# Marking three adjacency visits by one operation each, in a graph-transformer block on one Trainium2 core

## What is computed

```python
def gnn_layer(x, W, b, src, dst):
    h = x @ W.T + b
    msgs = h[src]
    agg = segment_sum(msgs, dst, num_segments=1250)
    return relu(agg)
...
xn = layernorm(x)
x = x + gnn(xn, edges, W1, b1, W2, b2) + mix(xn, Wq, Wk, Wv, W1, W2)
x = x + ffn(layernorm(x), gate_weight, experts)
```

## Time and profile before

| | us |
|---|---|
| median of 3 runs | 469.77 |
| lowest, highest | 468.29, 471.64 |
| the profiled execution | 468.61 |
| span of its trace | 466.8 |

### The profile page before, as it was taken

The page is one execution under the profiler, slowest core; times in us unless marked ns, Lnnn a source line. Parts: engine busy times, 40 slices in busy tenths (PEclk is TensorE's granted clock), DMA queues, the critical chain, the costliest instruction groups (busy, mean ns, idle before and its releaser), DMA issues.

```text
span 466.8 us, 6816 instructions
## 1 busy us (share of the span) xinstructions
PE 451.0 (97%) x2424; PEld 360.6 (77%) x2424; DVE 320.9 (69%) x1104; ACT 150.6 (32%) x272; POOL 63.1 (14%) x90
## 2 busy tenths in 40 slices
PE   7999999999999999999999999999999998878995
PEld 3788778888888888888779999877777776655783
DVE  6995699899998988897752110444645666777972
ACT  4686453322323332332222110222133114551110
POOL 4088200000000000000004000002300000006642
PEclk9999999999999999999999999999999999999999
DMA  8902002911000000001200000002744449305891
GB/s 219 287 1 91 1 0 91 219 50 65 2 1 1 1 1 1 1 2 20 108 0 4 1 1 1 1 0 53 277 139 134 134 142 380 131 1 190 289 356 71
DMA packets 20846, 40.46 MB, mean 87 GB/s; under 512 B 2953, under 2 KB 3283, under 8 KB 20805
## 3 DMA queue, kind: packets, MB, share of 16 engines
q1 hardware_dynamic: 18549, 32.55, 22.4%
q0 software_dynamic: 2256, 7.39, 4.5%
HBM read 30.10 MB, written 10.31 MB: 87 GB/s over the span
## 4 chain that ended last, share of the span: by engine, by line
PE 86%; DVE 8%; ACT 2%; issue 1%; DMA 1%; SPq 0%; POOLq 0%; DVEq 0%
PE ps L736 46%; PE ps L1031 9%; PE ps L957 9%; PE ps L848 5%; PE ps L723 5%; PE ps L1167 2%; ACT scrap_a L1424 1%; PE ps L1048 1%; PE ps L1137 1%; DMA X<-in_x 1%; PE ps L880 1%; PE ps L770 1%; PE ps L984 1%; PE ps L1008 1%; PE ps L1078 1%
## 5 line engine op out<-in xcount | busy, mean ns | idle before, releaser
L1713 DVE TENSOR_SCALAR RING_D<-places,PLACES 125x170 bf16<-125x170 f16 (+1 forms) x239 | 63.5, 266 | 0.0
L1714 DVE TENSOR_SCALAR RING_S<-iota,HOME 125x128 bf16<-125x128 f16 x239 | 60.4, 253 | 0.0
L957 PE MATMUL ps<-AT,H1H 125*128 125x416 f32 (+1 forms) x108 | 38.0, 352 | 0.0
L957 PE MATMUL ps<-AT,H1L 125*128 125x416 f32 (+1 forms) x108 | 38.0, 351 | 0.0
L1031 PE MATMUL ps<-H2H,AT 125*125 125x512 f32 x90 | 36.1, 402 | 0.0
L1031 PE MATMUL ps<-H2L,AT 125*125 125x512 f32 x90 | 35.5, 394 | 0.0
L1048 PE MATMUL ps<-WE0H 128*128 128x512 f32 x129 | 35.4, 408 | 0.0
L1781 DVE TENSOR_TENSOR ps<-ps,bias 125x512 f32<-125x512 f32 x20 | 14.0, 700 | 27.9 <-PE ps L736 27.9
L1860 DVE SCALAR_TENSOR_TENSOR ZL<-ps,ZH 128x416 fp32r<-128x416 f32 (+1 forms) x12 | 6.3, 585 | 38.7 <-ACT ZH L1369 38.7
L723 PEld LDWEIGHTS ps<-RING_D,RING_S 125*125 125x125 bf16 x239 | 25.7, 136 | 7.9
L605 POOL TENSOR_TENSOR G2L<-RAW_G,G2H 128x512 fp32r<-128x512 f32 x4 | 5.0, 1287 | 192.2 <-ACT G2H L1186 192.2
(11 more groups left out here) (410 smaller groups left out, 1171.7 us busy)
## 6 DMA issues: line engine op xcount, KB each, us to landing
RAW_E<-in_experts SPq DMA_DIRECT2D x8, 1024.0 KB, 9.9
RAW_AGAIN<-in_experts SPq DMA_DIRECT2D x3, 1024.0 KB
X<-in_x SPq DMA_DIRECT2D x1, 2240.0 KB
out_x<-X SPq DMA_DIRECT2D x10, 224.0 KB
scratch<-X SPq DMA_DIRECT2D x10, 224.0 KB
scratch<-Y SPq DMA_DIRECT2D x10, 224.0 KB
RAW_K<-in_WkT SPq DMA_DIRECT2D x4, 256.0 KB, 4.2
RAW<-in_mW2T SPq DMA_DIRECT2D x1, 1024.0 KB, 11.8
```

The source lines that it names most:

```text
L957: pe.matmul(place(f), h[0:TT, k, 128 * f:128 * (f + 1)], AT[0:TT, k, c0:c1], start=(k == 0 and n == 0), stop=False)
L1713: V.tensor_scalar(hot_d(v, width(b)), places[0:ET, 0:width(b)], PLACES[0:ET, c:c + 1], None, ALU.is_equal)
L1714: V.tensor_scalar(hot_s(v), iota[0:ET, :], HOME[0:ET, c:c + 1], None, ALU.is_equal).then_inc(done["marked"], 1)
```

## The change

Visits are put into sets. For block 0 a set is three visits of that block; after it, a set holds visit number s of each block of a group of three, so it has three members where all three blocks have that visit, else two or one. There are 104 sets (`NS`) for the 291 visits.

DVE writes all members of a set by two operations instead of two for each visit. The members lie interleaved: column h of member k is element 3h + k. So `hot_s` is [128, 3] and `hot_d` [170, 3], and the comparison is a TENSOR_TENSOR of a constant table (`iotas`, `spread`: each value three times) with the keys of the set, broadcast over the columns. Before it was a TENSOR_SCALAR with one key. `HOME` and `PLACES` become float16. Both operands of a visit's matmul are now read with a step of three bfloat16 elements, 6 bytes; before they were read without gaps. PE waits and raises its semaphore once per set.

The list of places changes with it: one set at each place of `vp`, `cp` and `h`, two sets at the start of each query product (none in its middle), and three at places 0 and 12 of each mixing tile (none at 6 and 18). The last set falls into `h8`; the last visit before was in `h7`. The rings hold 2 and 9 sets. The calls of `mark_next` on DVE follow, and GpSimd writes two tables more or wider.

```diff
-RING_A, RING_B = 6, 16
+RING_A, RING_B = 2, 9
...
+def mark_sets():
+    sets = [[(0, s) for s in range(o, min(o + SIDE, VISITS[0]))] for o in range(0, VISITS[0], SIDE)]
+    for g in range(NG):
+        blocks = range(max(SIDE * g, 1), min(SIDE * (g + 1), NB))
+        for s in range(VISITS[blocks[0]]):
+            sets.append([(b, s) for b in blocks if s < VISITS[b]])
...
-            spots += [(f"q{i}", 0, 4), (f"q{i}", 6, 4 if i % 4 == 1 else 3)]
+            spots += [(f"q{i}", 0, 2)]
         if i:
-            spots += [(f"x{i - 1}", n, 3 if n == 12 else 4) for n in (0, 6, 12, 18)]
-    spots += [(f"h{i}", 6, 3) for i in range(NT)]
+            spots += [(f"x{i - 1}", n, 3) for n in (0, 12)]
+    spots += [(f"h{i}", 6, 1) for i in range(NT)]
...
-            link(nc.gpsimd.iota(iota[:], [[1, 128]], base=0, channel_multiplier=0,
+            link(nc.gpsimd.iota(iotas[:], [[1, 128], [0, SIDE]], base=0, channel_multiplier=0,
+                                allow_small_or_imprecise_dtypes=True))
+            link(nc.gpsimd.iota(spread[:], [[1, W * NT], [0, SIDE]], base=1, channel_multiplier=0,
                                 allow_small_or_imprecise_dtypes=True))
...
                     pe.wait_ge(done["marked"], v + 1)
-                    pe.matmul(PS[4 + g % 2][0:TT, o:o + width(b)], hot_s(v)[:, 0:TT], hot_d(v, width(b)), start=(s == 0),
-                              stop=(s == VISITS[b] - 1), skip_group_check=True).then_inc(done["visited"], 1)
+                    for k, (b, s) in enumerate(SETS[v]):
+                        o = NT * (EDGES[b] - EDGES[SIDE * g])
+                        mm = pe.matmul(PS[4 + g % 2][0:TT, o:o + width(b)], hot_s(v)[:, 0:TT, k], hot_d(v)[:, 0:width(b), k], start=(k == 0 and (b, s) == (SIDE * g, 0)),
+                                       stop=(v in GROUP_ENDS and k == len(SETS[v]) - 1), skip_group_check=True)
+                    mm.then_inc(done["visited"], 1)
...
-                        V.tensor_scalar(hot_d(v, width(b)), places[0:ET, 0:width(b)], PLACES[0:ET, c:c + 1], None, ALU.is_equal)
-                        V.tensor_scalar(hot_s(v), iota[0:ET, :], HOME[0:ET, c:c + 1], None, ALU.is_equal).then_inc(done["marked"], 1)
+                        V.tensor_tensor(hot_d(v)[:, :, 0:m], spread[0:ET, :, 0:m], PLACES[0:ET, c:c + m].unsqueeze(1).broadcast_to([ET, W * NT, m]),
+                                        ALU.is_equal)
+                        V.tensor_tensor(hot_s(v)[:, :, 0:m], iotas[0:ET, :, 0:m], HOME[0:ET, c:c + m].unsqueeze(1).broadcast_to([ET, 128, m]),
+                                        ALU.is_equal).then_inc(done["marked"], 1)
```

More of the change, by code:

```diff
@@ L188 @@
 EDGES, COLUMN = block_columns()
-ORDER = [(b, s) for b in range(NB) for s in range(VISITS[b])]
+def mark_sets():
[4 more added lines that the diff above has]
+            sets.append([(b, s) for b in blocks if s < VISITS[b]])
+    assert sum(map(len, sets)) == NV
+    for one in sets:
+        assert [COLUMN[x] for x in one] == list(range(COLUMN[one[0]], COLUMN[one[0]] + len(one)))
+    return sets
+SETS = mark_sets()
+NS = len(SETS)
+GROUP_ENDS = {v: SETS[v][0][0] // SIDE for v in range(NS) if v == NS - 1 or SETS[v + 1][0][0] // SIDE > SETS[v][0][0] // SIDE}
 def visits_in_products():
-    spots = [("vp0", 6, 3)]
+    spots = [("vp0", 6, 1)]
     for u in ("vp1", "vp2", "vp3", "cp0", "cp1", "cp2", "cp3"):
-        spots += [(u, n, 3) for n in (0, 6)]
+        spots += [(u, n, 1) for n in (0, 6)]
     for i in range(NT + 1):
         if i < NT:
-            spots += [(f"q{i}", 0, 4), (f"q{i}", 6, 4 if i % 4 == 1 else 3)]
+            spots += [(f"q{i}", 0, 2)]
         if i:
-            spots += [(f"x{i - 1}", n, 3 if n == 12 else 4) for n in (0, 6, 12, 18)]
-    spots += [(f"h{i}", 6, 3) for i in range(NT)]
+            spots += [(f"x{i - 1}", n, 3) for n in (0, 12)]
+    spots += [(f"h{i}", 6, 1) for i in range(NT)]
     found, v = [], 0
     for unit, n, count in spots:
-        count = min(count, NV - v)
+        count = min(count, NS - v)
         if count:
@@ L209, in visits_in_products @@
         v += count
-    assert v == NV
+    assert v == NS
     return found
@@ L322, in gps_block @@
         tri = small("tri", [128, 128], F32, "a")
-        iota = small("iota", [128, 128], F16, "a")
         places = small("places", [128, HOTW], F16, "a")
-        HOME = small("HOME", [128, NV], F32, "a")
-        PLACES = small("PLACES", [128, NV], F32, "a")
+        HOME = small("HOME", [128, NV], F16, "a")
+        PLACES = small("PLACES", [128, NV], F16, "a")
+        spread = small("spread", [128, W * NT, SIDE], F16, "a")
         keys = at("keys", [128, 3, 2, ET], F16, areas["a"][0] / KB)
@@ L329, in gps_block @@
                   at("LEFT_0c", [128, 1, D], F32R, areas["a"][0] / KB)]
-        HOT_S = small("HOT_S", [128, RING_A, 128], BF16, "a")
+        HOT_S = small("HOT_S", [128, RING_A * SIDE * 128], BF16, "a")
+        iotas = small("iotas", [128, 128, SIDE], F16, "a")
+        iota = iotas[:, :, 0]
         edge = at("edge", [128, 2, 2, ET], F32, areas["a"][0] / KB)
-        HOT_D = small("HOT_D", [128, RING_A * W * NT], BF16, "a")
-        RING_S = at("RING_S", [128, RING_B, 128], BF16, 125)
-        RING_D = at("RING_D", [128, RING_B, W * NT], BF16, 129)
+        HOT_D = small("HOT_D", [128, RING_A * HOTW], BF16, "a")
+        RING_S = at("RING_S", [128, RING_B, 128, SIDE], BF16, 125)
+        RING_D = at("RING_D", [128, RING_B, W * NT, SIDE], BF16, 131.75)
         start = small("start", [128, NB + 1], F32, "a")
         turns = small("turns", [128, NB], F32, "a")
-        over = small("over", [128, 1], F32, "a")
-        grp = small("grp", [128, 2, 2], F32, "a")
+        over = small("over", [128, 1], F32, "k")
+        grp = small("grp", [128, 2, 2], F32, "k")
         eps = small("eps", [128, 2], F32, "a")
@@ L464, in hot_s, with hot_d @@
             r = ring_slot(v)
-            return HOT_S[0:ET, r, :] if r < RING_A else RING_S[0:ET, r - RING_A, :]
-        def hot_d(v, w):
+            if r >= RING_A:
+                return RING_S[0:ET, r - RING_A]
+            return HOT_S[0:ET, 128 * SIDE * r:128 * SIDE * (r + 1)].rearrange("p (h n) -> p h n", n=SIDE)
+        def hot_d(v):
             r = ring_slot(v)
-            return HOT_D[0:ET, W * NT * r:W * NT * r + w] if r < RING_A else RING_D[0:ET, r - RING_A, 0:w]
+            if r >= RING_A:
+                return RING_D[0:ET, r - RING_A]
+            return HOT_D[0:ET, W * NT * SIDE * r:W * NT * SIDE * (r + 1)].rearrange("p (d n) -> p d n", n=SIDE)
         def width(b):
@@ L713, in visits @@
                 for v in VISITS_AT.get((unit, n), ()):
-                    b, s = ORDER[v]
-                    g = b // SIDE
-                    if s == 0 and b % SIDE == 0:
+                    g = SETS[v][0][0] // SIDE
+                    if SETS[v][0] == (SIDE * g, 0):
                         if g < 2:
@@ L926, in tiles_again @@
                         pe.wait_ge(again[a], g * rounds + n + 1)
-                        pe.matmul(ps[:, 0:HOTW], HOT_S[0:ET, a, 0:TT], HOT_D[0:ET, HOTW * a:HOTW * (a + 1)],
+                        pe.matmul(ps[:, 0:HOTW], HOT_S[0:ET, 128 * a:128 * a + TT], HOT_D[0:ET, HOTW * a:HOTW * (a + 1)],
                                   start=(opening and a == 0), stop=False, skip_group_check=True).then_inc(again_used[a], 1)
@@ L1308, in groups_ending @@
                     for v in VISITS_AT.get((unit, n), ()):
-                        b, s = ORDER[v]
-                        if s == VISITS[b] - 1 and (b % SIDE == SIDE - 1 or b == NB - 1):
-                            store_counts(b // SIDE, v)
+                        if v in GROUP_ENDS:
+                            store_counts(GROUP_ENDS[v], v)
             def store_counts(g, v):
@@ L1753, in _ @@
                 context_left(c)
-                mark_next(2)
+                mark_next((2, 2, 1, 2)[c])
             for i in range(NT + 1):
-                if i < NT and i:
+                if i:
                     mark_next()
@@ L1759, in _ @@
                     add_mix(i - 2)
-                if i < NT and i:
-                    mark_next()
                 if i < NT:
@@ L1769, in _ @@
                     q_inverse(i)
-                if i:
-                    mark_next()
+                if i and i < NT:
                     mark_next()
```

11 lines of the change are left out of this document (4 added, 7 removed).

## The result

| | us |
|---|---|
| changed kernel, median of 6 runs | 478.71 (478.68 to 478.84) |
| before, median of 6 runs on the same chip | 469.1 (468.04 to 472.01) |
| ratio, 95% interval | 1.0218 (1.0195 to 1.0242) |
| span of the profiled execution | 477.0, before 466.8 |

A forecast was written before the change was run, and what follows sets the result against it. PE was taken to bound the kernel. 468.6 us less 1.0 for fewer runs plus 11.9 for the 6-byte step gave 479.5 for the profiled execution, 480.7 against the median of before; range 468.0 to 484.5 us.

The forecast's parts named there:

- rivals 1 and 2: Visits on PE: the first, 6-byte step free, 468.8 us, chance 0.26; the second, milder limit, 472.8 to 475.2 us, chance 0.12.
- rival 1: PE's visits: the 6-byte step is free, visits keep 75 ns, only fewer runs count, 468.8 us; chance 0.26.
- What bounds: Whole span: PE sets the time at 97% busy; some 35 us of relief on DVE is hidden and gives nothing.
- The price of a gapped column: PE's visits: 170 columns at 6 bytes take 116 ns, 41 ns more per visit, 11.9 us over 291 visits.
- the float32 row: Profile row of float32 matmuls, columns 4 bytes apart: 0.453 ns per column, read as 8.8 bytes per ns passed over.
- The bound above: Upper limit for a visit, from the routing product's 20-byte step: 1.8 ns per column, 310 ns per visit, 68 us more.
- The price of a run: Visits beside products on PE: 0.035 us per run stays; 83 runs become 54, 1.0 us less.
- Order, rings and waits, forecast at nothing: Marking order on DVE, smaller rings and PE's waits: sets are ready ahead of PE, so no cost.
- PE stays without idle time from 86 to 250 us: Sign expected in the changed profile: no idle time on PE between those times.
- The marking: DVE: 0.62 us per set, or 1.06 if short broadcast rows cost twice per element; DVE stays under PE.
- rival 4: DVE becomes the bound: marking four times dearer per element, 1.96 us per set, 60 us and more; chance 0.03.
- The start: GpSimd's tables: `iotas` 1.34, `spread` 1.73 us, covered; if rows of three cost more, the start slips by up to 2 us.

The follow-up runs named there:

- pairs of keys without the gap: Changed kernel with each key kept twice, so two operations per set write every member without gaps: 468.57 us, ratio 1.0017 against the kernel before.
- the kernel with the moving operand alone: Kernel before with its order and marking, only the visits' moving operand (170 columns) stored with the 6-byte step: 476.72 us, ratio 1.0182.
- the sweep: Kernel before, visits of six loop rounds reading 170 moving columns at steps of 2 to 12 bytes, output wrong: 75, 77, 117, 152, 190, 227 ns per visit.
- moving the call: Changed kernel with three sets for the first mixing tile marked behind the first query tile's inverse, not ahead of its maximum: 477.29 us, ratio 1.0191 against before.

## Why the prediction was right

The forecast was 480.7 us with a range of 468.0 to 484.5; 478.71 was measured. Of the 2.0 us between them 0.7 come from the base: the kernel before had 469.77 in three runs and 469.1 in six. The range is wide and takes in rivals 1 and 2, so that the time lies inside it says little. What speaks for the forecast is the 1.04 us of nine visits, which it had named against 0.68 for rival 1. Step by step, with what each term measured:

1. **What bounds.** Only PE carries the end, so DVE's relief is worth nothing: shown. DVE is busy with marking for 80 us in place of 103, PE had no idle time in the loop behind its first query tile, and pairs of keys without the gap came out level with before.
2. **The price of a gapped column.** 116 ns per visit was taken from the float32 row; the trace has 116. Shown by the kernel with the moving operand alone, and the sweep shows that the row was rightly carried over: what counts are the bytes passed over, up to 16 a step. That two rows five times apart in step gave nearly one rate, 8.8 and 11, was in part luck, since at 20 bytes a step the skipped bytes cost nothing. The bound above, 310 ns by the 20-byte row, was a saturated point of the same law.
3. **The price of a run.** Forecast: it stays, and 29 fewer runs give 1.0 us. Wrong in kind, and the largest error: where the moving operand is gapped the 0.035 us vanish for every run, 83 x 0.035 = 2.9 us in place of 1.0. Where it is not, it stays (2.83 with the stationary operand gapped or none). My reading is that the float32 load behind a run finds its cover under a matmul whose moving operand takes 116 ns but not under one of 75. The sweeps fit it: the price falls from 0.07 to 0 us as the moving operand takes longer, and stays at 0.025 to 0.045 when only the load of a visit does. That it is this load that waits was not tried by itself.
4. **Order, rings and waits, forecast at nothing.** One place failed: five sets stand ahead of the first maximum on DVE. The prediction asked whether PE finds its sets marked, not what DVE owes PE behind them. 1.2 us, shown by moving the call; so the sign "PE stays without idle time from 86 to 250 us" failed here.
5. **The marking.** 0.62 us per set forecast, 0.76 measured: rows of three keys cost 0.69 ns per element ((505 - 418) / 126) against 0.5. Free in the loop, since DVE stays under PE; in rival 4's direction, but far from it. The relief was 19 us of DVE's time and not 35, and DVE in 130 to 150 us is busy for 14.7 us and not for 12.
6. **The start.** `iotas` and `spread` took 1.95 and 2.52 us, not 1.34 and 1.73 (4.7 ns per element in rows of three, 3.1 in rows of six and ten), and the first transpose came at 7.42 us, not at 6.57. It was not the constants that passed this on: PE waits again at 11 us for rows of X in either kernel, and on the chain there stands the load of X, 0.33 us longer in this execution; the first visit came 0.36 us later. That load varies between executions whose start is the same program: 4.47 us before, 4.80 with both operands gapped, 5.04 with the stationary one.

The sum of the span: 11.9 - 2.9 + 1.2 + 0.4 = 10.6 us, against 10.2 measured; the 0.6 us of the products at 227 ns per matmul would bring it to 10.0. The forecast had 11.9 - 1.0 = 10.9. That it came so near is in part luck: two errors of opposite sign, 1.9 and 1.2 us, partly cancelled. Rival 1, the rule of two hits in a line, was the one to take seriously, and it fell by the 116 ns and by the sweep.

The Trainium skill, Advanced Engine Details and Errata (SBUF Cachelines), has lines of 16 bytes in SBUF and wants at least two hits in a line to absorb the latency. The runs agree on the lines: 60 columns cost the same at 16 and at 32 bytes a step. They differ on the hits: with two in a line (8 bytes) 170 columns take 152 ns, with two or three (6 bytes) 117, and only with four (4 bytes) 77 against 75.

## What to carry to other kernels

A layout that helps the engine that writes can tax the engine that reads, and the tax counts where the reader bounds. Before a matmul operand gets a gap, price it: the columns times the step, counted up to 16 bytes, over 8.8 bytes per ns, against 0.41 ns per column; for 2-byte data a step of two elements is nearly free (77 ns against 75), three are not (116). And where an in-order engine gets its work in larger pieces, look at what now stands behind each piece, not only at whether the pieces are ready in time.

## What the runs showed of the hardware that was not expected

- PE reads a moving operand at one price per 16 bytes touched, 1.8 ns, from 4 to 32 bytes a step (170 columns: 77 ns at 4 bytes, 227 at 12; 60 columns: 108 at 16, 112 at 32). The float32 matmuls of this kernel, 0.453 ns per column without gaps, lie on the same line, so they may be bounded by it too; that was not tried.
- The load of a stationary operand passes over memory faster: a visit grows by 21.5 ns for 250 bytes more, 11.6 bytes per ns against 8.8 to 9.0. It ran into a visit's time at 6 bytes already (83 ns against 75).
- The 0.035 us that a run of short bfloat16 matmuls costs between float32 ones vanish when the moving operand of the short ones takes 108 ns or more, and grow to 0.07 when it is 60 columns without gaps. A visit of 148 ns that is slow by its load leaves them as they are.
- A DVE comparison of 16-bit data takes 0.5 ns per element with broadcast rows of 2 keys (416 and 352 ns for 510 and 384 elements) and between the rows of 4 and 6 keys of the earlier trace rows, and 0.69 with rows of 3 (505 and 418 ns). Writing 2-byte results with a step of 6 bytes lengthens a TENSOR_SCALAR of 128 elements from 0.25 to 0.33 us, and one of 170 from 0.26 to 0.37.
